# The third layer's causal mask moved from four TensorE products a slot into VectorE's row-minimum instructions

## What is computed

```python
qkv = jnp.einsum('bsh,oh->bso', hidden_states, Wqkv)
xq, xk = rope(xq), rope(xk)
xk, xv = repeat(xk, 4), repeat(xv, 4)
scores = jnp.einsum('bqhd,bkhd->bhqk', xq, xk) / sqrt(128)
scores = jnp.where(causal, scores, -1e30)
probs = softmax(scores)
out = jnp.einsum('bhqk,bkhd->bqhd', probs, xv)
return out @ Wo.T
```

## Time and profile before

| | |
|---|---|
| median of 3 runs | 1495.88 us (1494.92 to 1500.24) |
| the profiled execution, span | 1490.3 us |
| its whole time | not listed; the median is 5.6 us above the span |
| TensorE busy over the span | 1394.3 us, 94% |
| VectorE busy | 999.2 us, 67% |
| ScalarE busy | 715.8 us, 48% |
| third layer's attention, slots with scores | from 648 to 1305 us |
| period of a middle slot there | 20.99 us |

### The profile page before, as it was taken

How to read it: one execution, slowest core, us unless ns; L and a number is a source line. 1 busy time by engine, 2 the same in 40 slices (tenths; PEclk the granted TensorE clock), 3 DMA queues, 4 the chain that set the end, 5 groups by cost and what they waited for, 6 DMA issues and landing times.

```text
span 1490.3 us, 25846 instructions
## 1 busy us (share of the span) xinstructions
PE 1394.3 (94%) x9284; PEld 1210.1 (81%) x9284; DVE 999.2 (67%) x1823; ACT 715.8 (48%) x1868; POOL 458.8 (31%) x359
## 2 busy tenths in 40 slices
PE   5999999899999797989999999999999999848998
PEld 4778887577777676789999999999999999837887
DVE  6577666589998645457666776667666776764554
ACT  5566666522222314156565565656565565522332
POOL 5221111122221732335243443425243443124000
PEclk9899999999999896999999999999999999969999
DMA  5010001132230002011102020201102020010000
GB/s 184 1 45 1 2 2 44 43 107 85 94 110 0 22 1 66 16 55 32 49 29 70 28 70 28 70 17 31 50 28 70 28 71 28 1 64 8 15 14 28
DMA packets 31237, 63.71 MB, mean 43 GB/s; under 512 B 4684, under 2 KB 5351, under 8 KB 31170
## 3 DMA queue, kind: packets, MB, share of 16 engines
q1 hardware_dynamic: 29938, 61.89, 12.8%
q10 hardware_dynamic: 1232, 0.93, 0.2%
HBM read 60.68 MB, written 2.13 MB: 42 GB/s over the span
## 4 chain that ended last, share of the span: by engine, by line
PE 83%; DVE 11%; issue 3%; ACT 2%; DMA 1%; POOL 0%; DVEq 0%; POOLq 0%; SPq 0%; ACTq 0%
PE PS L357 19%; PE PS L359 19%; PE PS L358 18%; PE PS L1680 3%; PE PS L1990 3%; PE PS L1976 2%; PE PS L1977 2%; PE PS L1975 2%; PE PS L1613 2%; PE PS L1700 2%; PE PS L1661 1%; PE PS L1633 1%; DVE F_t L1061 1%; PE PS L1696 1%; PE PS L1966 1%
## 5 line engine op out<-in xcount | busy, mean ns | idle before, releaser
L357 PE MATMUL PS<-XNH,E_WL 128*128 128x256 f32 x768 | 217.3, 283 | 0.8 <-DVEq L352 0.8
L358 PE MATMUL PS<-XNL,E_WH 128*128 128x256 f32 x768 | 217.1, 283 | 0.0
L359 PE MATMUL PS<-XNH,E_WH 128*128 128x256 f32 x768 | 217.0, 283 | 0.0
L559 POOL TENSOR_TENSOR E_sw<-E_sw,rope2s 128x1024 f32<-128x1024 f32 x64 | 103.9, 1624 | 280.3 <-ACT E_sw L611 280.3
L1375 DVE TENSOR_REDUCE E_nb<-PS 128x4 f32<-128x512 f32 x64 | 61.3, 958 | 181.6 <-PE PS L1977 181.6
L611 ACT ACTIVATE E_sw<-PS 64x256 f32<-64x256 f32 (+1 forms) x128 | 89.6, 700 | 125.5 <-PE PS L359 124.0
L357 PEld LDWEIGHTS PS<-XNH,E_WL 128*128 128x128 f32 x768 | 147.0, 191 | 2.5 <-DVEq L352 1.2
L358 PEld LDWEIGHTS PS<-XNL,E_WH 128*128 128x128 f32 x768 | 147.1, 192 | 1.3
L359 PEld LDWEIGHTS PS<-XNH,E_WH 128*128 128x128 f32 x768 | 147.1, 191 | 0.0
L467 POOL TENSOR_TENSOR E_WL<-raw,E_WH 128x512 fp32r<-128x512 f32 x80 | 109.9, 1403 | 105.0 <-ACT E_WH L611 104.4
L838 ACT ACTIVATE E_p<-PS,E_nb 128x128 f32<-128x128 f32 (+1 forms) x256 | 104.3, 420 | 32.9 <-DVE E_nb L1375 32.9
(11 more groups left out here) (287 smaller groups left out, 3979.1 us busy)
## 6 DMA issues: line engine op xcount, KB each, us to landing
raw<-in_w SPq DMA_DIRECT2D x97, 256.0 KB, 2.8
words<-in_words SPq DMA_DIRECT2D x11, 768.0 KB, 4.2
wo<-in_wo SPq DMA_DIRECT2D x32, 256.0 KB, 3.7
zb<-z_scratch SPq DMA_DIRECT2D x11, 384.0 KB, 4.8
scb<-in_scales SPq DMA_DIRECT2D x11, 384.0 KB, 5.5
X<-in_x SPq DMA_DIRECT2D x8, 256.0 KB, 6.1
out<-X SPq DMA_DIRECT2D x8, 256.0 KB, 2.1
wo<-in_w SPq DMA_DIRECT2D x4, 256.0 KB, 5.0
```

Source lines behind the costliest of these rows:

```text
L357: nc.tensor.matmul(o, sl, mh, start=first, stop=False, **shared)
L358: nc.tensor.matmul(o, sh, ml, start=False, stop=False, **shared)
L359: return nc.tensor.matmul(o, sh, mh, start=False, stop=last, **shared)
L559: nc.gpsimd.tensor_tensor(E_sw[:, heads, :], E_sw[:, heads, :], rope2s[:, :].unsqueeze(1).broadcast_to([P, heads.stop - heads.start, SEQ]) ...
```

## The change

The mask becomes a tile `mask_row` of 256 columns, 128 zeros and then the mask; `mask_ts` is its second half. The four mask products of each slot go, and the first score product of each bank starts the bank. On VectorE each `maxima` becomes a memset of one column and four instructions, one a head, that add the mask to the scores in place in PSUM and give the row minimum of the sum: for block 0 over 128 columns with the mask, for block 1 over 256 with zeros and mask. The last of the four signals. The scratch tile zq moves into the first third of `words0`.

```diff
-        mask_ts = keep("mask_ts", [P, P], BF16)
         mask01 = keep("mask01", [P, P])
+        mask_row = keep("mask_row", [P, 2 * P], BF16)
+        mask_ts = mask_row[:, P:2 * P]
...
-            zq = sb(early, "zq", [P, C], I32)
             z1 = sb(early, "z1", [NF, 3 * C], F16)
             words0 = sb(early, "words0", [P, 3, C], I32)
+            zq = words0[:, 0, :]
...
+                E_seen = sb(st, "E_seen", [P, 2])
...
-            for t, name in [(identb, "identb"), (mask_ts, "mask_ts"), (mask01, "mask01"), (shift_k, "shift_k"), (rope2c, "rope2c"), (rope2s, "rope2s")]:
+            for t, name in [(identb, "identb"), (mask01, "mask01"), (mask_row, "mask_row"), (shift_k, "shift_k"), (rope2c, "rope2c"), (rope2s, "rope2s")]:
...
                 def maxima(tb):
                     dve.wait_ge(e2["sc"], i * 2 + (tb - 1))
-                    V.tensor_reduce(E_nb[:, 4 * tb:4 * tb + 4],
-                                    PS[:, 3 + 2 * tb:5 + 2 * tb, :].rearrange("p n (h s) -> p (n h) s", h=2)[:, :, 0:(tb + 1) * P],
-                                    AXIS.X, ALU.min).then_inc(e2["least"], 1)
+                    V.memset(E_seen[:, tb:tb + 1], 0.0)
+                    for h in range(4):
+                        at = (h % 2) * SEQ
+                        seen = PS[:, 3 + 2 * tb + h // 2, at:at + (tb + 1) * P]
+                        last = V.tensor_tensor_reduce(seen, seen, mask_row[:, (1 - tb) * P:2 * P], 1.0, 3e38, ALU.add, ALU.min,
+                                                      E_nb[:, 4 * tb + h:4 * tb + h + 1])
+                    last.then_inc(e2["least"], 1)
...
-                    for tb in range(2):
-                        for n in range(2):
-                            seen = PS[:, 3 + 2 * tb + n, :].rearrange("p (h s) -> p h s", h=2)[:, :, tb * P:(tb + 1) * P]
-                            mm(seen, identb[:, :], mask_ts[:, :].unsqueeze(1).broadcast_to([P, 2, P]), start=True, stop=False,
-                               skip_group_check=True)
                     pe.wait_ge(e2["qlo"], i * 2)
...
-                            mm(o, QKL[:, h, t], QKH[:, 4, 0:seen], start=False, stop=False, skip_group_check=True)
+                            mm(o, QKL[:, h, t], QKH[:, 4, 0:seen], start=(h % 2 == 0), stop=False, skip_group_check=True)
```

More of the change, by code:

```diff
@@ L1695, in scores @@
                     seen = PS[:, 2 * tb + e, :].rearrange("p (h s) -> p h s", h=2)[:, :, tb * P:(tb + 1) * P]
-                    mm(seen, identb[:, :], mask_ts[:, :].unsqueeze(1).broadcast_to([P, 2, P]), start=True, stop=False, skip_group_check=True)
+                    mm(seen, identb[:, :], mask_ts.unsqueeze(1).broadcast_to([P, 2, P]), start=True, stop=False, skip_group_check=True)
                 for h in range(4):
@@ L2164 @@
         sc3=rows(a["L3_ffn_scale"][:, 0]), b3=rows(a["L3_ffn_bias"]),
-        ident=np.eye(P, dtype=f32), identb=np.eye(P, dtype=bf16), mask_ts=hidden.astype(bf16),
+        ident=np.eye(P, dtype=f32), identb=np.eye(P, dtype=bf16), mask_row=np.concatenate([np.zeros((P, P)), hidden], 1).astype(bf16),
         mask01=(hidden.T == 0).astype(f32),
```

## The result

The changed kernel takes **1482.57 us** (median of 4 runs, 1478.57 to 1484.23) against 1495.55 us for the kernel before (4 runs, 1494.92 to 1500.24). The ratio is 0.9917, with a 95% interval of 0.9899 to 0.9935, or 12.4 us gained. It is faster by more than 0.5%, a case to which I had given 0.34. The first rival, a small add-on, comes nearest with 1484.9 us. In a later round one execution of the kernel before took 4767 us; it was classed as slow and is in no ratio here.

What follows compares the result with a forecast made beforehand. TensorE was taken to bound the third layer's attention. Masks 11.8 us gained, less 3.9 of middle-slot stalls and 1.2 at the ends, make 6.7: 1495.88 - 6.7 = 1489.2 us, range 1484.0 to 1513.

Steps and rivals of the forecast that it cites:

- The first rival: VectorE's accumulator costs under 0.08 us a head, so no stall in middle slots: 11.0 gained, 1484.9 us; chance 0.33.
- The bound: Third layer's attention: the 30 middle slots go at TensorE's pace, so a TensorE instruction taken out is time gained.
- The masks' price: Four mask products a slot on TensorE, read from starts as 0.37 us (from above 0.48): 32 x 0.37 = 11.8 us gained.
- The add-on: e, the extra VectorE time a head for giving the accumulator beside a plain product: taken as 0.09 us, bounds 0 to 0.27.
- s goes through whole: s, block 1's added VectorE time (4e + 0.25 = 0.61 us), delays everything behind it, to the scaled E_p, in full.
- The slack: Middle slots: scaled E_p is ready 0.48 us before TensorE's transposes need it, counted at the fifth weight load.
- the term 30 x 0.13 = 3.9: TensorE's stall at the transposes of 30 middle slots, 0.13 us each as 0.61 exceeds 0.48: 3.9 us lost.
- my formula: Gain is 11.84 - 2s - 30(s - 0.48), without the last term where s is under 0.48; s = 4e + 0.25.
- The ends: First and last slot have no slack at the transposes, so VectorE's lateness counts in full: 2 x 0.61 = 1.2 us lost.
- The rest of the edit: Larger mask load, its changed place in SP's queue and zq inside words0: priced at nothing.
- Half rate: VectorE's new reduces take twice the time per column: s = 1.95, 36 us lost, 1532 us; chance 0.08.
- serialising: Each VectorE accumulator read waits for its product and holds the next, e = 0.20: 13.2 us lost, 1509 us; chance 0.20.

Runs made afterwards that it cites:

- The run with s = 0.62: Changed kernel with one more VectorE reduction, over 128 columns, ahead of block 1's reduces in each slot: 1481.86 us, ratio 0.992.
- The second profile: The changed kernel itself, run anew and profiled again: 1480.3 us (6 runs), ratio 0.9914, profiled span 1476.6 us.
- the kernels with a late VectorE: Changed kernel with one more VectorE reduction ahead of block 1's reduces: 1481.86 us with 128 columns, 1488.32 with 256, 1494.79 with 512.
- the two with the idle time filled: Unused products in the last slot: 20 added to the changed kernel, 1482.15 us; 18 added to the kernel with the first layer changed too, 1478.34 us.

## Why the prediction was right and wrong

- **The bound: right.** TensorE has no idle time in the stage, and a product removed is time gained. All middle slots shortened alike.
- **The masks' price: too small.** After "I take that for the lower bound too, since the next product can't have started late" I took this bound as the price, and that was a mistake: the first score product's start wasn't late, but its own step was long, 0.14 in place of 0.06. The term was 32 x 0.37 = 11.8 and measured 32 x 0.45 = 14.4, so 2.6 us more; my upper bound of 0.48 was the nearer one. (In the last slot, where TensorE starts after idling, the masks are worth only 0.36: the first score product steps 0.16 there without them too. That is 0.1 us in the sum.)
- **The add-on: too large, within its bounds.** I took e = 0.09 from ScalarE's read and measured 0.05; the memset at 0.07 showed no price. On VectorE's queue that is 0.35 in place of 0.61. "s goes through whole" was not quite so: E_nb is ready for ScalarE only behind the last read, and the second reciprocal waits for ScalarE, so at E_p the lateness is s = 0.42, not 0.35.
- **The slack: the step that failed.** The "0.48 us of slack", counted on the fifth weight load, is 0.64 counted where it decides, at the fifth product. The run with s = 0.62, my own forecast's size, had no lengthening, so the term 30 x 0.13 = 3.9 measured nothing, and would have done so with my own e. It had a second error: with the measured s of 0.42 a slack of 0.48 would have been enough as well. By my formula stalls begin at e = 0.10 (4e + 0.25 = 0.64) and not at 0.06, and the line between forecast and first rival, 7.5 us gained, moves from e = 0.08 to 0.12.
- **The ends: right.** No slack there; 2 x 0.42 = 0.8 in place of 1.2. TensorE's waits at L1991 of the first slot rose from 1.6 to 2.0 us.
- **The rest of the edit at nothing: right** (ratio 1.0004).
- **Half rate and serialising: not so.** The reduces of block 1 step 0.385 us, where serialising would have made 0.53 and half rate over 0.6. A 128-column difference costs 0.385 - 0.25 = 0.135 us, or 1.05 ns a column, the one-input rate that I had computed. The Trainium skill's sentence on accumulating two-source operations ("Vector Engine (DVE) Microarchitecture Reference", section "Points that are easy to get wrong") spares this pair of sources as worded. The trace shows the full rate, which agrees with it, but no run has the pair of sources that it warns of.

The account, mended: 32 x 0.45 - 2 x 0.42 = 13.6 us gained. The second profile's span fell by 1490.3 - 1476.6 = 13.7. That it comes so near is in part luck, since the spans of one kernel differ by some microseconds: the first profile's fell by 8.9, as 2.4 us went at half clock in its last slot, and 1.7 near 1355 us. The differences of the medians, 13.0 and 14.3 (the second without the execution of 4767 us), and the ratios (12.4 and 12.9 us) lie around it. From my 6.7 the way to 13.6 is 2.6 of masks, 3.9 of stalls and 0.4 of ends. The range was too narrow at its low end because it took in "a little of the 0.48" for the masks, when the step that followed them hadn't been read.

What stays open: the last 1 us or so of the kernel with both the masks and the new instruction; why it and the kernels with a late VectorE had the lower clock in so many executions; and what makes the clock fall in the last slot.

## What to carry to other kernels

Price a product on TensorE's path over the two products that follow it, not to the next start alone: what was removed may also have slowed its successor's step. Count slack at the product and not at the weight load, since the loads' lead is given up before any time is lost; and if the forecast hangs on a few tenths of slack, a run with one added instruction of known length measures it. If an instruction writes its result by a second, later record, count its consumers from the end of that record, on the other engines too. A step moved to an engine with cover is free only where the cover is there: free in the third layer's middle slots, while in the first layer TensorE's idle time rose by 11 us and the median fell by only 3.5.

## What the runs showed of the hardware

VectorE's reduce with an accumulator leaves two records, the reduce and a read of 143 ns, and the pair steps 0.25 us at 128 columns and 0.385 at 256, only about 0.05 more than a plain instruction, and less than ScalarE's 0.17 with its read the earlier trace rows. (The plain reduces of the late kernels, which read SBUF, step 0.22 and 0.34; against these it is 0.03 to 0.05.) ScalarE, which needs the result, starts 0.11 us behind the end of the last read. The reads as grouped by line, from 640 to 1305 us (busy time, mean ns of one):

```profile
L1381 DVE DVE_READ_ACCUMULATOR2_ANT E_nb<- 128x1 f32 x256 | 36.7, 143 | 0.0
```

The granted clock differed between executions of one and the same program: 0.72 over the 12 us of the last slot in one and 1.00 in another, after the same idle time of 2.34 and 2.35 us. Before the fall TensorE had stood idle, but so it had where no fall came. Three other profiles show the same fall in the last slot's scores: that of the kernel with only the masks out and both of the kernel with the first layer changed; the two with the idle time filled don't. The fall cost 2.4 us, so a difference of two profiled spans is only worth what the clock in both of them allows. The same holds for whole executions: with both the masks and the new instruction, one at a mean clock of 0.971 spanned 1492.0 us and one at 0.963 1503.6.

A weight load runs 0.23 us ahead of its product when nothing waits (885.16 and 885.39). When the load has to wait for its data, load and product start together (both 886.16), so a load could come 0.16 us late (0.64 - 0.48) and cost TensorE nothing.
